# Sums of squares added in pairs on GpSimd, weight splits cut in halves, and attention values as products of two heads

## The chip, the cores and the metric

One core of a Trainium2 chip runs the whole program in one launch. The metric is the device time of that core in microseconds. Five engines work side by side, each through its own list of instructions, and wait for one another on semaphores: TensorE (PE in the profile, its weight loads as PEld), VectorE (DVE), ScalarE (ACT), GpSimd (POOL) and SyncE (SP), which issues most of the DMAs.

## What is computed

Four layers over 4 sequences of 256 tokens with 256 features: a product with a context matrix whose operands are rounded to fp8, a feed-forward layer with ternary weights, a cross attention with int8-rounded weights (16 heads), and a block with grouped attention (32 query heads, 8 key and value heads, head size 64, causal) and a mixture of 16 experts. The change touches the second layer and the attention of the fourth. Cut to these two:

```python
def _L0_ffn_ref(x, w_gate_up, w_proj):          # x: layer norm of the residual
    gu = jnp.einsum('bsd,hd->bsh', x, ternary_quant(w_gate_up))
    gate, up = jnp.split(gu, 2, axis=-1)        # 1024 hidden features each
    h = jax.nn.silu(gate) * up
    hn = h * rsqrt(mean(h * h, -1) + eps)
    return jnp.einsum('bsh,dh->bsd', hn, ternary_quant(w_proj))

def _L1_ffn_ref(x, ...):                        # its attention
    q, k, v = h @ wq, h @ wk, h @ wv            # 32, 8, 8 heads of 64
    scores = einsum('bqhd,bkhd->bhqk', rope(q), rope(k)) / 8    # causal
    o = einsum('bhqk,bkhd->bqhd', softmax(scores), v)
    x = x + o @ wo
    ...
```

## The kernel before

All data that is worked on stays in SBUF, most of it in one large tensor, `arena`, whose stretches are named by hand. Every engine's order is written out by hand in its own block (`sync`, `gpsimd`, `scalar`, `vector`, `tensor`); a semaphore is raised by the instruction that makes a value and waited for by those that use it.

**The first feed-forward layer.** The tokens are taken in two chunks of 512 (`CHUNKS`), the 1024 hidden features in 8 blocks of 128 (`J0`). That gives 16 units `u`, chunk `u // 8`, block `u % 8`. In a unit:
- TensorE (`gate_and_up`, line 1743) makes gate and up of the block, 8 products of 512 columns, in two of four PSUM banks. It waits until the product of unit u-2 is formed.
- ScalarE takes the silu of gate (line 937), and then for the unit before (`h0_hi`) rounds the product to float16 (line 928) and squares it (line 931) into a ring of two, `h_sq`.
- VectorE multiplies silu by up into `h0` (line 1320).
- GpSimd subtracts the rounded half from the product (line 733), which gives the low half.
- TensorE sums the squares of unit u-2 over the features (`sum_squares`, line 1752): for each of 4 token tiles a product of the 128x128 squares, as the weights, with a column of ones. In float32 that is two records each.

After unit 9 stands the down product of chunk 0 (`ffn0_down(0)`, line 1765, 64 products of 256 columns), which needs the low halves of units 0 to 7; after the last sums stands that of chunk 1. At unit 11 VectorE takes the mean square of chunk 0 (`mean_square`, line 1308), GpSimd raises it to the power -1/2 (line 744; in GpSimd's list this stands after unit 9's operations), and VectorE scales and adds the down product to the residual (`add_ffn0`, line 1299) and takes statistics (line 1132). For chunk 1 the same follows after VectorE's rounding of the int8 weights of the next layer (`q8`, lines 1156 to 1173).

Within the same units five pieces of the fourth layer's weights (`FW = 5`, 2048 columns each) are loaded into two staging buffers and split into a float16 high and low half. SyncE issues the load of piece i (line 632) when the split of piece i-2 is done. GpSimd makes the high half (line 739, "the cast") in the units `FW_AT = [4, 6, 8, 10, 12]`, behind the unit's subtraction; VectorE makes the low half (line 1328, "the split") two units later (`FW_LAG`), behind the unit's product. The lists in question:

```python
            for i in range(FW):
                if i == 0:
                    sp.wait_ge(w0_cast, 2 * PIECES)
                if i >= 2:
                    sp.wait_ge(fw_ready, i - 1)
...
                if u == J0 + 3:
                    mean_square(0)
                    add_ffn0(0)
                if u - FW_LAG in FW_AT:
```

**The grouped attention** has 64 units (`UNITS`): batch, group of 4 query heads (`GH`) that share a key and value head, and query tile `t` of 128 tokens; with causal masking tile 0 sees one key tile and tile 1 two. In step i TensorE does, in this order: `a_turn(i-2)` (transposes of the weights of attention, line 1982), `a_score(i)` (lines 1965 to 1967), a projection of later tokens (line 1800), `a_values(i-2)` (line 1999) and `out_projection(i-3)` (line 2015). `a_values` multiplies, for each pair of heads, key tile and head in the pair, a 128x64 block of values, as weights, with 128 columns of `apt`; even heads fall on the lower 64 partitions of PSUM bank 5, odd ones on the upper 64. All of it is float32, two records for each product.

## Time and profile before

| | us |
|---|---|
| median of 3 runs | 794.15 (793.99 to 794.79) |
| the profiled execution | 799.23 |
| its span, first to last instruction | 797.4 |

Mean granted clock of TensorE over the span: 0.917 of full speed. Engines' busy times: TensorE 632.0, VectorE 557.4, GpSimd 463.4, ScalarE 431.2 us.

Times in the views are microseconds from the start of the span, with durations in ns where said. A line of a timeline is: start, duration, engine, source line, operation, output <- input by the program's names, size, count of the instructions merged, and in brackets the idle time of the engine before it and what ended that. A matmul's record ends when the modelled pipeline is through; the next one of its kind starts earlier.

### The profile page before, as it was taken

The page shows a single profiled execution, that of the slowest core. Times are in us where ns is not written, and L with a number is a line of the kernel's source. Part 1 is how long each engine was busy: PE and PEld are TensorE (multiplying, and loading weights), DVE is VectorE, ACT ScalarE, POOL GpSimd, SP SyncE. Part 2 cuts the span into 40 slices and gives each one's busy share as a digit, 9 for nine tenths or more (in the row PEclk, how much of TensorE's full clock was granted, in tenths as well). Part 3 has the DMA queues.
Part 4 walks back from the last instruction along what each step waited for, and adds up shares of the span by engine and source line. Part 5 has one row for each costly group of instructions (what it writes and reads, how often), then busy time and mean ns, then how long its engine had stood idle before and what let it go on. Part 6 is the DMA issues. An engine that isn't in the chain of part 4 may idle for free.

```text
span 797.4 us, 16336 instructions
## 1 busy us (share of the span) xinstructions
PE 632.0 (79%) x5656; PEld 441.5 (55%) x5656; DVE 557.4 (70%) x1420; ACT 431.2 (54%) x1213; POOL 463.4 (58%) x424
## 2 busy tenths in 40 slices
PE   0247999468888844689999999999887789999970
PEld 0124667246566533367777777677675436666640
DVE  5999558868878976856677577677656765555445
ACT  4823532059768820456576666666654217777640
POOL 1051654248977942269698788768532336777750
PEclk9778896789999976989999999999999979999995
DMA  9500130127536530024042332422500913333428
GB/s 299 189 1 1 49 110 1 53 79 221 168 118 207 158 121 1 0 54 80 15 89 46 93 55 42 67 28 50 177 15 8 401 47 96 105 108 109 103 84 263
DMA packets 83466, 77.99 MB, mean 98 GB/s; under 512 B 49408, under 2 KB 75776, under 8 KB 82880
## 3 DMA queue, kind: packets, MB, share of 16 engines
q1 hardware_dynamic: 78880, 64.33, 28.0%
q0 software_dynamic: 4512, 12.71, 5.5%
q8 instruction: 42, 0.69, 0.4%
q14 instruction: 32, 0.26, 0.1%
HBM read 47.46 MB, written 18.55 MB: 83 GB/s over the span
## 4 chain that ended last, share of the span: by engine, by line
PE 52%; DVE 24%; ACT 7%; POOL 7%; issue 6%; DMA 2%; SPq 1%; POOLq 0%; ACTq 0%; DVEq 0%
PE ps L1800 10%; PE ps L2093 8%; PE ps L2015 5%; PE ps L1999 5%; PE ps L1982 5%; PE ps L2116 4%; ACT arena L974 2%; PE ps L1765 2%; PE ps L1857 2%; DVE arena L1496 2%; PE ps L1743 2%; POOL arena L832 2%; DVE tiny L1489 2%; PE ps L1724 2%; ACT arena L1059 1%
## 5 line engine op out<-in xcount | busy, mean ns | idle before, releaser
L1059 ACT ACTIVATE arena<-ps,tiny 128x128 f32<-128x128 f32 (+1 forms) x256 | 104.2, 419 | 53.6 <-DVE tiny L1489 53.6
L832 POOL TENSOR_TENSOR arena<-arena,tiny 128x512 f32<-128x512 f32 x64 | 93.9, 1467 | 62.9 <-DVE tiny L1500 62.6
L1496 DVE COPY arena<-ps 128x512 f32<-128x512 f32 x64 | 44.3, 691 | 75.3 <-PE ps L1982 75.3
L2093 PE MATMUL ps<-arena 128*128 (+1 forms) x282 | 68.7, 380 | 1.0 <-DVE arena L1640 0.5
L1800 PE MATMUL ps<-arena,xt_hi 128*128 128x512 f16 (+1 forms) x224 | 64.2, 372 | 3.6 <-DVE xt_lo L1278 3.0
L867 POOL DMA_INDIRECT arena<-h_store,arena x47 | 46.0, 979 | 33.5 <-DVE arena L1619 19.5
L1999 PE MATMUL ps<-arena 128*64 128x128 f32 x768 | 56.1, 280 | 11.3 <-DVE arena L1504 11.3
L1489 DVE TENSOR_REDUCE tiny<-ps 128x4 f32<-128x512 f32 x64 | 60.9, 952 | 1.3 <-PE ps L1967 0.9
L1999 PEld LDWEIGHTS ps<-arena 128*64 128x64 f32 x768 | 41.4, 136 | 32.3 <-issue 23.1
L1633 DVE SCALAR_TENSOR_TENSOR ps<-ps,arena 128x256 f32<-128x256 f32 x47 | 20.3, 433 | 55.4 <-ACT arena L1111 55.4
L1965 PE MATMUL ps<-arena 128*128 128x128 f16 (+1 forms) x256 | 58.5, 247 | 0.2 <-ACT arena L1038 0.2
L1967 PE MATMUL ps<-arena 128*128 128x128 f16 (+1 forms) x256 | 58.5, 247 | 0.0
L873 POOL DMA_INDIRECT y_store<-arena x47 | 46.4, 987 | 20.1 <-issue 12.2
L974 ACT ACTIVATE arena<-arena 128x256 f32<-128x256 f32 x128 | 54.6, 506 | 2.7 <-DVE arena L1395 2.6
L2015 PE MATMUL ps<-arena 128*128 128x256 f16 x384 | 53.0, 274 | 2.6 <-DVE xn L1511 2.4
L1982 PE MATMUL ps<-ident,arena 128*128 128x128 f32 x384 | 53.0, 274 | 2.3 <-POOL arena L832 2.3
L820 POOL TENSOR_TENSOR arena<-arena 128x512 f16<-128x512 f32 x36 | 41.7, 1158 | 21.2 <-ACT arena L1028 11.8
L1059 ACT ACTIVATION_READ_ACCUMULATOR arena<-ps,tiny 128x1 f32 x256 | 52.0, 203 | 0.0
L1966 PE MATMUL ps<-causal,ident_bf 128*128 128x128 bf16 x256 | 51.6, 220 | 0.0
L826 POOL TENSOR_TENSOR arena<-arena 128x512 f32<-128x512 f32 x34 | 43.2, 1270 | 7.3 <-DVE arena L1471 7.1
L1395 DVE CUSTOM_DVE_ANT_0 arena<-ps,arena 128x256 f32<-128x256 f32 x128 | 46.6, 420 | 0.0
L1982 PEld LDWEIGHTS ps<-ident,arena 128*128 128x128 f32 x384 | 43.4, 141 | 5.7 <-POOL arena L832 5.1
(295 smaller groups left out, 1738.4 us busy)
## 6 DMA issues: line engine op xcount, KB each, us to landing
e_store<-arena SPq DMA_DIRECT2D x13, 768.0 KB, 4.3
arena<-e_store SPq DMA_DIRECT2D x13, 768.0 KB, 9.4
work<-w_dram SPq DMA_DIRECT2D x27, 256.0 KB, 4.6
xn<-w_dram SPq DMA_DIRECT2D x21, 256.0 KB, 4.7
arena<-w_gate_up_t_dram SPq DMA_DIRECT2D x2, 1024.0 KB, 8.9
arena<-wq_dram SPq DMA_DIRECT2D x2, 1024.0 KB, 7.4
arena<-wo_dram SPq DMA_DIRECT2D x2, 1024.0 KB, 5.8
work<-y_store SPq DMA_DIRECT2D x8, 256.0 KB, 5.2
```

The source lines that it names most:

```text
L832: nc.gpsimd.tensor_tensor(p, p, arec[:, u % 4, :].unsqueeze(2).broadcast_to([P, GH, L]), ALU.mult)\
L974: nc.scalar.activation(xp[:, i % 2, h, :], masked[:, i % 2, h, :], ACT.Exp, bias=xnm[:, i % 4, h:h + 1], scale=-1.0).then_inc(x_exp, 1)
L1059: nc.scalar.activation(ap_[u % 3][:, h, 0:L], head_scores(u, h), ACT.Exp, bias=anm[:, u % 4, h:h + 1], accum_out=asum[:, u % 4, h:h + 1]). ...
L1489: nc.vector.tensor_reduce(anm[:, u % 4, :].rearrange("p (m h) -> p m h", m=u % TB + 1), scores, AX.X, ALU.max, negate=True).then_inc(a_max, 1)
L1496: nc.vector.tensor_copy(apt[:, u % 2, 0, :], ps[:, 3, :]).then_inc(a_pt, 1)
L1800: last = mm(dst, l, r, start=(n == 0), stop=(n == 3 * len(pairs) - 1))
L1965: mm(dst, q, kat[b % 2][:, g, 0:L], start=True, stop=False)
L1967: last = mm(dst, q, kbt[b % 2][:, g, 0:L], start=False, stop=True)
L1982: last = nc.tensor.transpose(ps[:, 3 + k, h * P:(h + 1) * P], ap_[u % 3][:, h, k * P:(k + 1) * P], ident[:, :])
L1999: last = mm(ps[half * HD:(half + 1) * HD, 5, pair * P:(pair + 1) * P], av[b % 2][:, k, g * HD:(g + 1) * HD], apt[:, u % 2, k, h * P:(h + 1 ...
L2015: last = mm(ps[:, 6, t * D:(t + 1) * D], l, r[:, g * 2 + o, :], start=first, stop=final)
L2093: last = mm(ps[:, 2 + i % 2, :], xg[:, i % 2, x_half * KB + k, :], weights(hidden_weights(slot, w_half, k), i), start=(n == 0), stop=(n == 5))
```

## The change

Three edits.

1. ScalarE squares into a ring of four (`h_sq` moves to another stretch of `arena`). After every second unit's subtraction GpSimd adds the squares of the two units, in place. `sum_squares` takes pairs: 8 calls instead of 16, at the units 4, 6, ... 14; pair 6 follows the last unit, and pair 7 stands inside the second down product, after its second token tile.
2. VectorE's split of a weight piece becomes two instructions of 1024 columns: the first two units after the cast, the second three units after, each behind what else VectorE does in its unit. The count of `fw_ready` doubles: SyncE waits for both halves of the piece whose buffer it fills.
3. `a_values` takes both pairs of heads in one product: 256 columns in two strided blocks of 128, instead of two products of 128. The order becomes key tile, then even and odd heads.

```diff
@@ -222,9 +222,9 @@
 
         h_hi, h_lo = ([c0([J0, CHUNK], F16), t[:, :, :].rearrange("p t d -> p (t d)").bitcast(F16)
                        .rearrange("p (j n) -> p j n", j=J0)] for t in (work, work2))
-        h_sq = c0([2, CHUNK], F32)
         w_sg = c0([PIECES, 2048], BF16)
         silu0 = c0([2, CHUNK], F32)
+        h_sq = carver(36864, 38912)([4, CHUNK], F32)
         h0 = carver(0, 4096)([J0, CHUNK], F32)
 
 
@@ -382,6 +382,7 @@
         h0_hi_ready = sem("h0_hi_ready")
         h0_split = sem("h0_split")
         h0_squared = sem("h0_squared")
+        squares_added = sem("squares_added")
         ms_out = sem("ms_out")
         ffn0_out = sem("ffn0_out")
         ms0_ready = sem("ms0_ready")
@@ -627,7 +628,7 @@
                 if i == 0:
                     sp.wait_ge(w0_cast, 2 * PIECES)
                 if i >= 2:
-                    sp.wait_ge(fw_ready, i - 1)
+                    sp.wait_ge(fw_ready, 2 * (i - 1))
                 for dst, src in stage_parts(a, i):
                     sp.dma_start(dst, src).then_inc(stage_loaded[i % 2], 16)
             sp.wait_ge(ffn0_added, CHUNKS)
@@ -732,6 +733,10 @@
                 pool.wait_ge(h0_hi_ready, u + 1)
                 nc.gpsimd.tensor_tensor(h_lo[c][:, j, :], h0[:, j, :], h_hi[c][:, j, :], ALU.subtract)\
                     .then_inc(h0_split, 1)
+                if u % 2:
+                    pool.wait_ge(h0_squared, u + 1)
+                    nc.gpsimd.tensor_tensor(h_sq[:, u % 4 - 1, :], h_sq[:, u % 4 - 1, :], h_sq[:, u % 4, :], ALU.add)\
+                        .then_inc(squares_added, 1)
                 if u in FW_AT:
                     i = FW_AT.index(u)
                     pool.wait_ge(w0_ready, PIECES)
@@ -926,9 +931,9 @@
             def h0_hi(u):
                 act.wait_ge(h0_ready, u + 1)
                 nc.scalar.activation(h_hi[u // J0][:, u % J0, :], h0[:, u % J0, :], ACT.Copy).then_inc(h0_hi_ready, 1)
-                if u >= 2:
-                    act.wait_ge(ms_out, u - 1)
-                nc.scalar.activation(h_sq[:, u % 2, :], h0[:, u % J0, :], ACT.Square).then_inc(h0_squared, 1)
+                if u >= 4:
+                    act.wait_ge(ms_out, u // 2 - 1)
+                nc.scalar.activation(h_sq[:, u % 4, :], h0[:, u % J0, :], ACT.Square).then_inc(h0_squared, 1)
 
             for u in range(U0):
                 act.wait_ge(gate_up, u + 1)
@@ -1304,7 +1309,7 @@
                     stat(c * TC + t, x)
 
             def mean_square(c):
-                vec.wait_ge(ms_out, (c + 1) * J0)
+                vec.wait_ge(ms_out, (c + 1) * J0 // 2)
                 nc.vector.tensor_scalar(ms0, ps[:, 6 + c, 0:TC], 1.0 / H0, FFN_EPS, ALU.mult, ALU.add)\
                     .then_inc(ms0_ready, 1)
                 vec.wait_ge(inv0_ready, c + 1)
@@ -1322,11 +1327,14 @@
                 if u == J0 + 3:
                     mean_square(0)
                     add_ffn0(0)
-                if u - FW_LAG in FW_AT:
-                    i = FW_AT.index(u - FW_LAG)
-                    vec.wait_ge(fw_hi_ready, i + 1)
-                    nc.vector.scalar_tensor_tensor(stage_target(i, False), stage[:, i % 2, :], WS,
-                                                   stage_target(i, True), ALU.mult, ALU.subtract).then_inc(fw_ready, 1)
+                for part in range(2):
+                    if u - FW_LAG - part in FW_AT:
+                        i = FW_AT.index(u - FW_LAG - part)
+                        cols = slice(part * 1024, (part + 1) * 1024)
+                        vec.wait_ge(fw_hi_ready, i + 1)
+                        nc.vector.scalar_tensor_tensor(stage_target(i, False)[:, cols], stage[:, i % 2, cols], WS,
+                                                       stage_target(i, True)[:, cols], ALU.mult, ALU.subtract)\
+                            .then_inc(fw_ready, 1)
                 if u < 4:
                     next(projection_steps, None)
             vec.wait_ge(xw_loaded, 64)
@@ -1745,12 +1753,13 @@
                             n += 1
                 last.then_inc(gate_up, 1)
 
-            def sum_squares(u):
-                c, j = u // J0, u % J0
-                pe.wait_ge(h0_squared, u + 1)
+            def sum_squares(pair):
+
+                c, j = pair // (J0 // 2), pair % (J0 // 2)
+                pe.wait_ge(squares_added, pair + 1)
                 for t in range(TC):
-                    last = mm(ps[:, 6 + c, t:t + 1], h_sq[:, u % 2, t * P:(t + 1) * P], ones_col[:, :],
-                              start=(j == 0 and t == 0), stop=(j == J0 - 1 and t == TC - 1))
+                    last = mm(ps[:, 6 + c, t:t + 1], h_sq[:, 2 * pair % 4, t * P:(t + 1) * P], ones_col[:, :],
+                              start=(j == 0 and t == 0), stop=(j == J0 // 2 - 1 and t == TC - 1))
                 last.then_inc(ms_out, 1)
 
             def ffn0_down(c):
@@ -1766,15 +1775,16 @@
                                       w_bf[:, 2, j * D:(j + 1) * D], start=(n == 0), stop=(n == 2 * J0 - 1))
                             n += 1
                     last.then_inc(ffn0_out, 1)
+                    if c and t == 1:
+                        sum_squares(U0 // 2 - 1)
 
             for u in range(U0):
                 gate_and_up(u)
-                if u >= 2:
-                    sum_squares(u - 2)
+                if u >= 4 and u % 2 == 0:
+                    sum_squares(u // 2 - 2)
                 if u == J0 + 1:
                     ffn0_down(0)
-            sum_squares(U0 - 2)
-            sum_squares(U0 - 1)
+            sum_squares(U0 // 2 - 2)
             ffn0_down(1)
 
             pe.wait_ge(ffn0_added, CHUNKS)
@@ -1915,7 +1925,7 @@
             pe.wait_ge(xo_added, T)
             transpose_tokens(3, work)
             pe.wait_ge(xt_ready, 16)
-            pe.wait_ge(fw_ready, FW)
+            pe.wait_ge(fw_ready, 2 * FW)
             def project(n):
                 b, c, t, _ = SIDE[n]
                 past = [m for m in range(n) if SIDE_BANK[m] == SIDE_BANK[n]]
@@ -1992,13 +2002,11 @@
                     pe.wait_ge(a_pt2, u // 2 + 1)
                 if u:
                     pe.wait_ge(a_o_read, u)
-                for pair in range(GH // 2):
-                    for k in range(t + 1):
-                        for half in range(2):
-                            h = pair * 2 + half
-                            last = mm(ps[half * HD:(half + 1) * HD, 5, pair * P:(pair + 1) * P],
-                                      av[b % 2][:, k, g * HD:(g + 1) * HD], apt[:, u % 2, k, h * P:(h + 1) * P],
-                                      start=(k == 0), stop=(k == t))
+                for k in range(t + 1):
+                    pairs = apt[:, u % 2, k, :].rearrange("p (a half q) -> p a half q", half=2, q=P)
+                    for half in range(2):
+                        last = mm(ps[half * HD:(half + 1) * HD, 5, 0:2 * P], av[b % 2][:, k, g * HD:(g + 1) * HD],
+                                  pairs[:, :, half, :], start=(k == 0), stop=(k == t))
                 last.then_inc(a_o, 1)
 
             def out_projection(u):
```

## Rows read from the trace of the kernel before

**Rows 1.** The page, part 1: busy us, share of the span, instructions.

```profile
PE 632.0 (79%) x5656; PEld 441.5 (55%) x5656; DVE 557.4 (70%) x1420; ACT 431.2 (54%) x1213; POOL 463.4 (58%) x424
```

**Rows 2.** Busy time by stretch: stretch, us, each engine busy (instructions), clock, DMA.

```profile
99.40:130.00 30.60, 27.94 (x175) 19.96 (x175) 20.77 (x24) 12.20 (x23) 19.27 (x12) 0.88 0.24 75
345.00:615.00 270.00, 253.20 (x2527) 191.89 (x2525) 183.45 (x370) 171.82 (x646) 194.00 (x153) 1.00 0.29 60
```

**Rows 3.** The chain that ended last, 110 to 146 us: start, us, what.

```profile
113.58 1.03 POOL inv L744
...
140.32 0.89 DVE x L1299 x2
```

**Rows 4.** Timeline of TensorE in the first feed-forward layer.

```profile
99.42 7.15 PE L1765 MATMUL ps<-arena 128*128 128x256 bf16 x64 [0.81 <-POOL arena L733]
...
110.67 0.95 PE L1752 MATMUL ps<-ones_col,arena 128*128 128x1 f32 x8
...
121.25 1.70 PE L1752 MATMUL ps<-ones_col,arena 128*128 128x1 f32 x8
...
130.41 9.87 PE L1765 MATMUL ps<-arena,work 128*128 128x256 bf16 x64
```

**Rows 5.** Timeline of GpSimd in the first feed-forward layer.

```profile
88.85 1.16 POOL L733 TENSOR_TENSOR arena<-arena 128x512 f16<-128x512 f32 x1 [1.38 <-ACT arena L928]
...
98.12 1.16 POOL L733 TENSOR_TENSOR arena<-arena 128x512 f16<-128x512 f32 x1
99.23 3.21 POOL L733 TENSOR_TENSOR work<-arena,work 128x512 f16<-128x512 f32 x1
...
117.57 1.15 POOL L733 TENSOR_TENSOR work<-arena,work 128x512 f16<-128x512 f32 x1
...
121.85 1.89 POOL L739 TENSOR_SCALAR arena<-arena 128x2048 f16<-128x2048 f32 x1
...
127.38 2.27 POOL L733 TENSOR_TENSOR work<-arena,work 128x512 f16<-128x512 f32 x2 [2.52 <-ACT work L928]
```

**Rows 6.** Timeline of VectorE in the first feed-forward layer.

```profile
98.19 3.24 DVE L1328 SCALAR_TENSOR_TENSOR arena<-arena 128x2048 f16<-128x2048 f32 x1 [1.61 <-POOL arena L739]
...
109.57 3.26 DVE L1328 SCALAR_TENSOR_TENSOR arena<-arena 128x2048 f16<-128x2048 f32 x1
112.76 0.68 DVE L1320 TENSOR_TENSOR arena<-ps,arena 128x512 f32<-128x512 f32 x1
...
116.33 1.41 DVE L1132 BATCH_NORM_STATS2 stats<-x 128x6 f32<-128x256 f32 x4
...
126.94 0.68 DVE L1320 TENSOR_TENSOR arena<-ps,arena 128x512 f32<-128x512 f32 x1
127.54 1.74 DVE L1161 TENSOR_REDUCE wamax<-arena 128x6 f32<-128x1536 f32 x1
...
138.08 0.88 DVE L1299 SCALAR_TENSOR_TENSOR x<-ps,inv,x 128x256 f32<-128x256 f32 x2 [1.14 <-POOL inv L744]
```

**Rows 7.** Timeline of SyncE's queue, 111 to 142 us.

```profile
112.86 0.37 SPq L632 DMA_DIRECT2D arena<-wo_dram  x1
```

**Rows 8.** The page, part 6: DMAs by name, KB each, us to landing.

```profile
arena<-wo_dram SPq DMA_DIRECT2D x2, 1024.0 KB, 5.8
```

**Rows 9.** Groups by line and form, 345 to 615: busy us, mean ns.

```profile
L1999 PE MATMUL ps<-arena 128*64 128x128 f32 x768 | 56.1, 280 | 11.3 <-DVE arena L1504 11.3
...
L2015 PE MATMUL ps<-arena 128*128 128x256 f16 x383 | 52.9, 274 | 2.6 <-DVE xn L1511 2.4 <-DVE arena L1504 0.2
...
L826 POOL TENSOR_TENSOR arena<-arena 128x512 f32<-128x512 f32 x34 | 43.2, 1270 | 7.3 <-DVE arena L1471 7.1
...
L1965 PE MATMUL ps<-arena 128*128 128x128 f16 x124 | 22.4, 219 | 0.0
```

**Rows 10.** Busy time of a stretch; its granted clock comes before DMA.

```profile
129.20:136.02 6.82, 6.82 (x34) 5.20 (x35) 6.65 (x23) 1.13 (x2) 0.46 (x1) 0.50 0.00 1
```

**Rows 11.** Timeline of TensorE: one unit of values with two key tiles.

```profile
612.49 1.09 PE L1999 MATMUL ps<-arena 128*64 128x128 f32 x16 [1.54 <-DVE arena L1504]
```

## The prediction

> **What bounds the kernel now.** I read the page first: TensorE is busy 79% of the span, GpSimd 58% [rows 1]. A share is a mean over stages, so next comes the table by stretch. The edits touch two: the first feed-forward layer (68 to 143 us), and the grouped attention (345 to 615 us), where TensorE is busy 253.2 of 270 us [rows 2], so only TensorE time counts there. In the first layer no engine is full, so I read the chain of waits: it runs through GpSimd's power at 113.58 and, after the second down product, VectorE's last additions at 140.32 [rows 3]. Then the timelines, engine by engine. The reader is to see four things.
>
> First, TensorE waits for GpSimd at the first down product (0.81 us, then 7.15 us of work) [rows 4]. GpSimd stands on the path by unit 7 already.
>
> Second, GpSimd and VectorE exclude each other in some pairs of operations. A subtraction takes GpSimd 1.16 us, but the one at 99.23 took 3.21 and ended at 102.44, 1.0 us after VectorE's split (98.19 to 101.43); that split in turn took 3.24 us, having waited for the subtraction of 98.12 to end at 99.28, so it needs some 2.15 alone [rows 5, 6]. I count each GpSimd operation and each split as holding one shared turn.
>
> Third, the last weight piece. Its load is issued at 112.86, when split 2 (109.57 to 112.83) is done, and lands 5.8 us later, at 118.7; its cast begins at 121.85, so the load is covered with 3.1 us to spare [rows 5 to 8].
>
> Fourth, the end: VectorE computes the eight tensors of the int8 weights from 127.54, is ready at 138.08, and adds the last pair of tiles at 140.32, after TensorE [rows 3, 6]. So VectorE's slack is about 1.4 us.
>
> **The change part by part.** *Squares in pairs.* TensorE issues 64 instead of 128 one-column records: eight groups fewer. A group of 8 spans 0.95 us at 2.4 GHz, some 0.8 of it not hidden, and 1.70 at the lower clock [rows 4]. That is 6 to 7 us of TensorE work, but this engine waits in this layer, so the work leaves only if nothing else is late. Added are eight additions of 128x512 float32 on GpSimd; no such addition runs in this layer, the nearest row is the float32 addition in attention, 1.27 us each [rows 9]. Bounds: 1.16 (the mixed subtraction) and 1.5 (with some exclusion on top). I take 1.27. Of these, the one after unit 3 has cover: GpSimd stood idle 1.38 us before 88.85 [rows 5]. The one after unit 5 delays subtraction 7, for which the first down product waits; the missing sums bring TensorE's units forward, and the split cut in two lets GpSimd in between. I work out +0.5 us for the start of that product (between 0 and +1.3).
>
> *Split in halves.* Split 2 becomes part 0 at unit 10 and part 1 at unit 11. Product 11, at 112.76 now behind the whole split [rows 6], starts half a split earlier: 112.3 with the +0.5 above. But part 1 stands in VectorE's order behind the mean square, the four additions and the four statistics of unit 11. Those additions need the inverse from GpSimd, whose power now stands behind the addition of squares 8 and 9 (112.3 to 113.6), so it starts at 113.6, as before (113.58). The statistics end at 117.7 as before [rows 3, 6]. Part 1 then waits for subtraction 11 to end (117.57 + 1.15 = 118.7 [rows 5]) and runs 1.1 us: done at 119.9, where split 2 was done at 112.83. SyncE issues the last load only then: **7.1 us later**. Nothing else is queued behind it on SyncE until the layer's end. It lands at 119.9 + 5.8 = 125.7. The cast of 121.85 starts at 125.9: **+4.0 us**, a new wait. Queued behind it on GpSimd: subtractions 13, 14, 15 and the additions of squares; waiting for it on VectorE: split 4, with product 15 behind its first part.
>
> The sum from there, in turns of the shared resource: cast 1.9 (127.8), subtraction 13 1.15 (128.9), split 4 part 0 1.1 (130.0; product 15 then, 126.94 before, +3.1), addition 13 1.27 (131.3), part 1 1.1 (132.4), subtractions 14 and 15 2.3 (134.7). Before, subtraction 15 ended at 127.38 + 2.27 = 129.65 [rows 5]: **+5.0**. The second down product starts at 134.8, where it started at 130.4 behind the last sums: +4.4. It lasted 9.87 us [rows 4], of which 5.6 at the lower clock, since 129.2 to 136.0 is granted 0.50 [rows 10]. TensorE will stand idle for longer before it than it did, so I give it no more of the full clock than it had. Inside it now stands one group of sums: +0.8. TensorE's end: 134.8 + 9.9 + 0.8 = 145.5, against 130.41 + 9.87 = 140.28: +5.2. VectorE, from 132.4 instead of 127.54, is ready for its last pair at 138.08 + 4.85 + 0.9 = 143.8 and is covered. So the layer ends **5.2 us later**. If the down product ran wholly at 2.4 GHz (7.15 us as the first one [rows 4]), VectorE would end it at 143.8: +3.5. If it ran wholly at the lower clock (about 14.3 + 1.6): +10. After it comes the layer norm on VectorE with every engine waiting, so nothing gives this back.
>
> *Values as products of two heads.* The records of that line fall from 768 to 384, each twice as wide. A unit of 16 takes 1.09 us, a record every 0.055 us [rows 11]. What a record costs is seen from its kind: 128 float32 columns last 280 ns, about as long as 256 float16 columns (274), while 128 float16 columns last 219 [rows 9]. A float32 column costs two; 128 of them hold their part of the array 256/2.4 = 107 ns. As one starts every 55 ns, the two halves of the output (64 columns each) are at work side by side. Afterwards 8 records hold their half 512/2.4 = 213 ns each, two at a time: 4 x 0.213 = 0.85 against 8 x 0.107 = 0.86. Only the 1 to 2 ns between records fall by half: 10 ns less for each of 32 units with two key tiles, 5 ns for the other 32, 0.5 us. Bounds: 0 and, if the offset of one half against the other grows with the record, +3; I take -0.4.
>
> A rule speaks otherwise. By the Trainium skill, "TensorE: Matmul & The Clock Gate", section "LDWEIGHTS (loading the stationary operand)", a weight load takes its columns divided by 1.2 GHz, 53 ns for 64; by that rule 16 loads in line fill 0.85 us, and the trace's loads of a unit fit that as well as the streams do. If loads are the limit, halving them pays; that is the first rival, which is priced from rows below.
>
> **Sum.** +5.2 - 0.4 = +4.8 us. The profiled execution takes 799.23 us (span 797.4 and 1.8 around it), 5.1 above the median of the runs, 794.15. The difference is carried over: profile 804.0, median 794.15 + 4.8 = **799.0 us**.
>
> **The rivals.** *Loads are the limit in attention (faster).* Then a unit of 16 saves 8 x 0.055 = 0.44 us and one of 8 saves 0.22: 32 x 0.66 = 21 us of TensorE. The line is busy 56.1 us and TensorE is full 94% of the stretch, so of the 21 perhaps half to two thirds reach the end, as other engines become late: -10 to -14. With +4.8 from the first layer: about 787. For it: the fit at 55 ns. Against it: the equal times of 128 float32 and 256 float16 columns, which the rule does not give. It decides from 5 us of attention saved. Chance 0.10.
>
> *The load is not late (no change).* If part 1 of split 2 came before the additions in effect, or the load landed in 3 us, the cast would start at 122.5; the adds would cost 2 x 1.27 less what the halves release early, and TensorE's lighter load would pay the rest: the layer at -1 to +1.5, 793 to 795.7. Against it: the order of the statements is fixed. Chance 0.15.
>
> *The clock.* The adds leave TensorE idle for longer, and the second down product, or units 14 and 15 also, run at the lower clock throughout: +8 to +10 in the layer, 801 to 804. Chance 0.15.
>
> *The exclusion does not bind the addition of squares*, or the halves slip between: +3 to +4, 797 to 798; within my case.
>
> **How the numbers follow.** My case, 796.5 to 801: 0.58. The clock: 0.15. No change: 0.15. Loads: 0.10, and 0.02 for neither. The likeliest is 799.0. The range takes in my case, the clock's and part of the no-change case: 793.8 to 803.0, leaving out loads (0.10) and the edges (0.08). A measurement can tell about 0.2% (1.6 us) from no change. Slower by more, above 795.7: 0.76. Faster by more, below 792.6: 0.12. Same: 0.12.
>
> **What would show it.** In the changed profile: the last load issued at about 120 instead of 112.86, and VectorE's split 2 part 1 just before it; GpSimd's last cast at about 126, after idle time that ends with a DMA; the additions of squares at about 1.27 us; the second down product starting near 134.8; the last pair of additions near 145.5. In attention: 384 records of about 0.38 us, a unit of 8 in about 1.1 us, and the stretch from the projections to the last product as long as now within 1 us. I am wrong if the last load is issued before 116, if a unit of values takes under 0.8 us, or if subtraction 15 ends by 131.

## The result and the profile after

The changed kernel takes 801.68 us, median of 7 runs (797.76 to 803.08), against 794.79 us (793.99 to 796.69) for the kernel before on the same chip: a ratio of 1.0079, interval 1.0059 to 1.0100, which is +6.3 us (4.7 to 8.0). Timed again with the experiments below the ratio is 1.0068 (1.0044 to 1.0092), +5.4 us. The prediction was 799.0 us, +4.8, with a range of 793.8 to 803.0; the median lies in the range, 2.7 above its middle value. Two executions, one of the kernel before at 1281 us and one of the kernel "values, casts on ScalarE" at 2137 us, are in none of the ratios.

The medians hide a shape. In the timings with the experiments 11 of 35, 6 of 34 and 6 of 24 executions of the kernel before took over 797.5 us, the others 793 to 797; of the 19 of after one took 797.8, two took 796.5, and 16 took 800 or more. The lowest times are only 3.6 to 3.8 us apart (793.99 and 797.76, 792.83 and 796.46). So part of the 5 to 6 us may be that executions of 798 us and more become the rule; the mean granted clock of an execution doesn't sort them (the kernel before took 799.47 at 0.928 and 792.96 at 0.919), and what does is not shown.

The first profile of the changed kernel took 802.12 us (span 800.3), only 2.9 more than the profile of before, 799.23. Both kernels were therefore profiled a second time: 795.64 us (span 793.8) for before, 804.8 (span 802.9) for after. One profile of either kernel differs from the next by 2 to 4 us, so sizes are taken from all of them. Part 1 of the page of after, to be set against [rows 1], and its part 5 for the values:

```profile
PE 625.4 (78%) x5208; PEld 414.6 (52%) x5208; DVE 561.2 (70%) x1425; ACT 431.2 (54%) x1213; POOL 477.4 (60%) x432
...
L2008 PE MATMUL ps<-arena 128*64 128x256 f32 x384 | 55.6, 394 | 11.4 <-DVE arena L1512 11.4
```

TensorE is busy 6.6 us less and the kernel is slower. GpSimd does 14.0 us more. By line, GpSimd in the first layer (60 to 150 us; columns as in [rows 9]), after and then before:

```profile
L738 POOL TENSOR_TENSOR arena<-arena 128x512 f32<-128x512 f32 x8 | 16.0, 2002 | 0.0
L734 POOL TENSOR_TENSOR work<-arena,work 128x512 f16<-128x512 f32 x8 | 11.9, 1488 | 6.1 <-ACT work L933 6.1
```

```profile
L733 POOL TENSOR_TENSOR work<-arena,work 128x512 f16<-128x512 f32 x8 | 12.9, 1620 | 8.1 <-ACT work L928 8.1
```

Eight additions of squares take 16.0 us, 2.0 each and not 1.27. The distribution of that line says why: 1.26 us at the least, 2.25 in the median.

```profile
L738 POOL TENSOR_TENSOR arena<-arena x8: 1261/2246/2252, 79.4 to 133.2; 128x512 f32<-128x512 f32 x8
```

Five of the six long ones stand beside half a split of VectorE. The sixth, that of unit 1, stands beside an operation of VectorE with two inputs in `arena` (start, length, engine, line), and ends 1.13 us after it:

```profile
79.37 2.25 POOL L738 TENSOR_TENSOR arena<-arena 128x512 f32<-128x512 f32 x1
```

```profile
79.04 1.45 DVE L1219 TENSOR_TENSOR arena<-arena 128x2048 bf16<-128x2048 bf16 x1
```

The chain of waits of after, from the power to the end of the layer (start, length, what; [rows 3] are its answers in before):

```profile
113.33 1.02 POOL inv L749
...
114.38 1.67 DVE x L1304 x4
...
117.44 2.11 DVE arena L1335
...
119.57 5.08 DMA arena<-wo_dram
...
124.80 1.90 POOL arena L744
126.70 1.12 POOL work L734
127.82 2.21 POOL arena L738
130.03 3.22 POOL work L734 x2
133.25 0.14 issue
133.38 6.55 PE ps L1774 x32
139.94 0.79 PE ps L1761 x8
140.72 3.53 PE ps L1774 x32
...
144.28 0.89 DVE x L1304 x2
```

The reader is to see the predicted path, link by link: power, additions of unit 11, part 1 of split 2, then a DMA that was not in the chain of before in this layer, the last cast, three subtractions with an addition between them, the second down product with a group of sums inside. The timelines confirm the two waits: SyncE issues the last load at 119.57 (112.86 in before [rows 7]; the line below merges it with the load issued at 101.28 and ends with it at 119.94), and GpSimd is idle 2.03 us for it.

```profile
101.28 18.66 SPq L633 DMA_DIRECT2D arena<-wo_dram  x2
```

```profile
124.80 1.90 POOL L744 TENSOR_SCALAR arena<-arena 128x2048 f16<-128x2048 f32 x1 [2.03 <-DMA arena<-wo_dram]
```

All the kernels' profiles side by side, in microseconds after the layer's first product (the one at 68.14 in the profile of before); "end" is the end of the layer's last statistics. The first three rows are one and the same layer, since the edit of the values does not touch it; they show how far two profiles of one thing lie apart. Where ScalarE casts, "last cast" is the start of the second half; the first half starts at 48.0 and at 53.8.

| kernel | first down product | last load issued | last cast | subtraction 15 ends | second down product | end | runs, ratio to before |
|---|---|---|---|---|---|---|---|
| before | 31.3 | 44.7 | 53.7 | 61.5 | 62.3 | 74.5 | |
| before, again | 29.6 | 43.0 | 52.0 | 59.7 | 60.8 | 71.9 | 1.0024 (0.9999 to 1.0048) |
| values alone | 31.8 | 45.3 | 54.3 | 62.1 | 62.7 | 75.1 | 1.0003 (0.9975 to 1.0031) |
| **after** | 30.0 | 51.4 | 56.6 | 65.1 | 65.2 | 78.4 | 1.0079 (1.0059 to 1.0100) |
| **after, again** | 30.4 | 51.7 | 57.2 | 65.6 | 65.8 | 77.9 | 1.0068 (1.0044 to 1.0092) |
| halves alone | 31.7 | 51.1 | 56.5 | 63.7 | 64.2 | 76.1 | 1.0026 (0.9999 to 1.0052) |
| pairs alone | 30.0 | 43.7 | 54.3 | 62.8 | 62.9 | 75.8 | 1.0063 (1.0043 to 1.0083) |
| pairs alone, narrow additions | 28.6 | 42.2 | 51.4 | 59.1 | 59.2 | 71.4 | 0.9999 (0.9978 to 1.0020) |
| after, halves early | 30.0 | 46.3 | 55.8 | 64.2 | 64.4 | 76.5 | 1.0027 (1.0004 to 1.0050) |
| after, narrow additions | 28.9 | 49.9 | 55.3 | 62.7 | 62.9 | 75.4 | 1.0032 (1.0012 to 1.0052) |
| after, both | 26.7 | 40.8 | 48.3 | 56.7 | 56.8 | 69.9 | 1.0015 (0.9992 to 1.0037) |
| values, casts on ScalarE | 28.6 | 42.0 | 50.4 | 58.4 | 59.4 | 71.2 | 0.9994 (0.9970 to 1.0019) |
| after, casts on ScalarE | 28.4 | 48.1 | 56.3 | 65.0 | 65.1 | 78.3 | 1.0070 (1.0044 to 1.0095) |

The span less this layer's length is 720.8 to 723.4 us in twelve of the thirteen profiles, and 725.0 in the second one of after. So the differences between profiles are made in this layer. But an old profile has to be chosen with care: those of "before" and "values alone" took 799.2 and 799.9 us, some 4 above the medians of their kernels, and have layers of 74.5 and 75.1; "before, again" took 795.6, like the median, and has 71.9. Beside after's 78.4 (an execution of 802.1, median 801.7) the layer grew by 6.5 us, which is all of the loss; against the mean of the three old profiles it is 4.3.

### The profile page after: what moved, and what is told of

Read it like the earlier page. It is cut to its first block, busy times and chain, and to the rows that moved or that the text cites. A ratio compares the mean times of both kernels' runs of the same rounds, so it can differ in the third digit from the quotient of the medians.

```text
span 800.3 us, 15453 instructions
## 1 busy us (share of the span) xinstructions
PE 625.4 (78%) x5208; PEld 414.6 (52%) x5208; DVE 561.2 (70%) x1425; ACT 431.2 (54%) x1213; POOL 477.4 (60%) x432
## 4 chain that ended last, share of the span: by engine, by line
PE 50%; DVE 26%; POOL 9%; ACT 7%; issue 5%; DMA 2%; SPq 1%; POOLq 0%; DVEq 0%; ACTq 0%
PE ps L1810 9%; PE ps L2101 8%; PE ps L2023 5%; PE ps L1992 5%; PE ps L2008 5%; PE ps L2124 4%; PE ps L1774 2%; ACT arena L979 2%; PE ps L1867 2%; DVE arena L1504 2%; POOL arena L837 2%; DVE tiny L1497 2%; ACT arena L1064 1%; PE ps L2113 1%; PE ps L2076 1%
## 5 line engine op out<-in xcount | busy, mean ns | idle before, releaser
L2008 PE MATMUL ps<-arena 128*64 128x256 f32 x384 | 55.6, 394 | 11.4 <-DVE arena L1512 11.4
L1992 PE MATMUL ps<-ident,arena 128*128 128x128 f32 x384 | 53.0, 274 | 2.3 <-POOL arena L837 2.3
L1976 PE MATMUL ps<-causal,ident_bf 128*128 128x128 bf16 x256 | 51.7, 220 | 0.0
L2023 PEld LDWEIGHTS ps<-arena 128*128 128x128 f16 x384 | 32.3, 98 | 30.2 <-issue 26.8
L1867 PE MATMUL ps<-ident,arena 128*128 128x128 f32 x256 | 37.1, 292 | 13.0 <-DVE arena L1423 8.3
```

Of the source, the lines that this page charges most:

```text
L1992: last = nc.tensor.transpose(ps[:, 3 + k, h * P:(h + 1) * P], ap_[u % 3][:, h, k * P:(k + 1) * P], ident[:, :])
L2008: last = mm(ps[half * HD:(half + 1) * HD, 5, 0:2 * P], av[b % 2][:, k, g * HD:(g + 1) * HD], pairs[:, :, half, :], start=(k == 0), stop=(k ...
L2023: last = mm(ps[:, 6, t * D:(t + 1) * D], l, r[:, g * 2 + o, :], start=first, stop=final)
```

## The experiments

**One edit at a time.** The theory: the loss is made in the first layer, by the additions' turns and by the last load; the values change nothing. The rivals: the values gain or cost microseconds (weight loads are the limit, or the two halves of the output stop overlapping), or one of the two edits in the layer costs all of it. First the values alone:

```diff
-                for pair in range(GH // 2):
-                    for k in range(t + 1):
-                        for half in range(2):
...
+                for k in range(t + 1):
+                    pairs = apt[:, u % 2, k, :].rearrange("p (a half q) -> p a half q", half=2, q=P)
+                    for half in range(2):
```

> The kernel before with the third edit alone: values of attention as products of two heads, 256 columns. My theory (a float32 record of 256 columns costs what two of 128 do): -0.5 us, between -1 and +1, and in the profile 384 records of about 0.38 us, a unit of two key tiles in 1.1 us. Rival A (this edit makes part of the slowdown, because the halves of the array work side by side for less of the time): +2 us or more, a unit above 1.2 us. Rival B (weight loads are the limit): -10 us, a unit of 0.7 us.

Measured: 795.87 us against 795.51, ratio 1.0003. The line's records take 55.6 us instead of 56.1, and the stretch from the first to the last of them is 261.7 us here and in both profiles of after, where it is 262.0 in both of before: -0.3 us, as worked out. Busy time of the weight loads of this line in attention, before and after:

```profile
L1999 PEld LDWEIGHTS ps<-arena 128*64 128x64 f32 x768 | 41.4, 136 | 32.3 <-issue 23.1 <-DVE arena L1496 9.2
```

```profile
L2008 PEld LDWEIGHTS ps<-arena 128*64 128x64 f32 x384 | 23.7, 135 | 35.9 <-issue 23.2 <-DVE arena L1504 9.3
```

384 loads are gone and the time stays, so they lay under the streams. By the rule of the Trainium skill ("TensorE: Matmul & The Clock Gate", section "LDWEIGHTS (loading the stationary operand)") a load takes its columns over 1.2 GHz; an estimate by it is 0.85 us for the 16 loads of a unit and 0.43 for 8. The unit went from 1.09 us to 1.08, so loads at that price are not what bounds it: the trace speaks against the first rival of the prediction.

The splits in halves alone:

```diff
-                if u - FW_LAG in FW_AT:
-                    i = FW_AT.index(u - FW_LAG)
...
+                for part in range(2):
+                    if u - FW_LAG - part in FW_AT:
```

> The kernel before with the second edit alone: splits in halves, the second part of split 2 behind the additions and statistics of unit 11. My theory (the last load is issued late and the last cast waits for it): +2.5 us (1.5 to 3.5), the last load issued at about 119 instead of 112.9, GpSimd idle before the last cast with a DMA as what ended it. Rival (only the additions of squares on GpSimd cost time): 0, and a gain of up to 1 us since product 15 no longer stands behind a whole split.

Measured: ratio 1.0026, +2.1 us (0 to 4); the medians lie 3.5 us apart, 798.98 and 795.51, and 11 of the 12 executions took over 798, while the lowest, 793.40, is 0.5 above the lowest of before. The theory of the expectation came out: the load at 119.52 us, GpSimd idle 2.71 us before the cast and released by the DMA, and the cost in the range. The last load is issued 51.1 us into the layer, as late as in after, and the last cast starts at 56.5, as in after. By the ratio this is a third of the loss, with a wide interval. So the late load, which the prediction made the origin of nearly all of it, is most likely not that by itself.

The squares in pairs alone:

```diff
+                if u % 2:
+                    pool.wait_ge(h0_squared, u + 1)
+                    nc.gpsimd.tensor_tensor(h_sq[:, u % 4 - 1, :], h_sq[:, u % 4 - 1, :], h_sq[:, u % 4, :], ALU.add)\
+                        .then_inc(squares_added, 1)
```

> The kernel before with the first edit alone: squares added in pairs on GpSimd, splits whole. My theory (additions take turns with VectorE's splits and stand ahead of subtractions that TensorE waits for): +3 us (1.5 to 5), the last load issued near 113 and the cast not waiting for it; the second down product starts some 3 us later than in the kernel before. Rival (the late load alone makes the slowdown): 0 or a gain of 1 us, from TensorE's lighter load.

Measured: ratio 1.0063, +5.0 us (3.4 to 6.6), the top of the range expected, with no load late (43.7). The second down product starts at 62.9, some 2 later than in the second profile of before and 1 later than the mean of the three, not the 3 us expected. Its additions wait for whole splits, where those of after wait for halves: 3.31 us in the median. GpSimd from 87 to 100 us of this kernel (start, length, engine, line, operation):

```profile
87.82 1.91 POOL L744 TENSOR_SCALAR arena<-arena 128x2048 f16<-128x2048 f32 x1
89.70 1.15 POOL L734 TENSOR_TENSOR arena<-arena 128x512 f16<-128x512 f32 x1
90.81 3.31 POOL L738 TENSOR_TENSOR arena<-arena 128x512 f32<-128x512 f32 x1
94.09 1.16 POOL L734 TENSOR_TENSOR arena<-arena 128x512 f16<-128x512 f32 x1
95.21 1.89 POOL L744 TENSOR_SCALAR arena<-arena 128x2048 f16<-128x2048 f32 x1
```

From cast to cast pass 7.39 us. The casts of before in the same stretch:

```profile
96.26 1.90 POOL L739 TENSOR_SCALAR arena<-arena 128x2048 f16<-128x2048 f32 x1
...
102.41 1.89 POOL L739 TENSOR_SCALAR arena<-arena 128x2048 f16<-128x2048 f32 x1
```

They are 6.15 us apart, and that is full already: a cast of 1.90, a split of 2.15 and two subtractions of 1.16 are 6.4 us of turns, less the hundredths by which records overlap. An addition of 1.26 comes on top: 7.4. The layer has three such cycles from cast to cast, 7.37 to 7.39 us here and 6.15 to 6.17 in before: 3.7 us of the loss.

**The additions' price.** In the next run they keep their place, their waits and their order, but have 32 columns instead of 512; the kernel leaves out the sums of the other columns:

```diff
-                    nc.gpsimd.tensor_tensor(h_sq[:, u % 4 - 1, :], h_sq[:, u % 4 - 1, :], h_sq[:, u % 4, :], ALU.add)\
+                    nc.gpsimd.tensor_tensor(h_sq[:, u % 4 - 1, 0:32], h_sq[:, u % 4 - 1, 0:32], h_sq[:, u % 4, 0:32], ALU.add)\
```

> The kernel before with the squares added in pairs, splits whole and values as before, and the additions narrowed from 512 columns to 32 (the rest of the sum is left out). It prices the time of eight additions where no load is late. If the additions cost by the time that they hold the turn shared with VectorE, the ratio falls from 1.0063 for the full additions to 0.998 to 1.002, since TensorE's lighter load (64 records fewer) is then free of charge. Rival, the waits by pairs (squares reach TensorE two units later, one group of sums inside the second down product): the ratio stays at 1.004 or above.

Measured: ratio 0.9999 where the full additions gave 1.0063. Eight times 1.01 us of GpSimd, 8 us, make some 5.1 us of the kernel. The cycles from cast to cast are 6.35 to 6.38 us again. What is left of the edit, the waits by pairs and TensorE's 64 fewer records, comes to nothing together (-1.8 to +1.6 us); the run doesn't part them, so a small cost of the one and a small gain of the other may cancel. The "6 to 7 us of TensorE work" in any case don't appear in the time. GpSimd in this kernel, and one split of VectorE:

```profile
89.33 1.16 POOL L734 TENSOR_TENSOR arena<-arena 128x512 f16<-128x512 f32 x1
90.44 2.30 POOL L738 TENSOR_TENSOR arena<-arena 128x32 f32<-128x32 f32 x1
92.70 1.16 POOL L734 TENSOR_TENSOR arena<-arena 128x512 f16<-128x512 f32 x1
```

```profile
89.39 3.24 DVE L1333 SCALAR_TENSOR_TENSOR arena<-arena 128x2048 f16<-128x2048 f32 x1 [1.28 <-POOL arena L744]
```

This is the turn at its plainest. The split is issued at 89.39, behind the subtraction of 89.33; it works when that ends, at 90.49, for 2.15 us, and ends at 92.63. The addition of 32 columns takes 0.25 us where nothing stands in its way; here it takes 2.30 and ends 0.11 us after the split. By the Trainium skill, "SBUF — State Buffer", section "Who interferes with whom", a VectorE instruction with two SBUF inputs contends with a GpSimd instruction that reads SBUF, and the port pair that they share is an exclusive lock. The trace agrees, to a tenth of a microsecond.

The same narrowing in the changed kernel:

> The changed kernel with GpSimd's additions of squares narrowed from 512 columns to 32; it leaves out the sum of the squares for the other columns of one unit in each pair, and every instruction, order and wait stays. It prices the time of the additions apart from their order. If the time that an addition holds the turn shared with VectorE is a cost of its own beside the late load, the additions last some 0.1 to 0.3 us, the power starts near 112.3 (113.33 in the changed kernel), subtraction 15 ends 1.5 to 2.5 us sooner than 133.2, and the ratio to the kernel before falls from 1.008 to about 1.005. Rival, the late load alone: it is still issued near 119, the cast still starts near 124.5, and the ratio stays at 1.008. Rival, the additions alone: the ratio falls to that of the halved splits by themselves, 1.0026, or below.

Measured: ratio 1.0032, so -2.9 to -3.7 us against the two timings of after. Subtraction 15 ends at 131.3, 1.9 sooner, as the theory had it; the late load alone (1.008) falls, the additions alone (1.0026) are within the interval, and so is the 1.005 that the theory gave. The load is still late (49.9), and GpSimd, with less to add, waits for it longer than in after.

```profile
123.92 1.90 POOL L744 TENSOR_SCALAR arena<-arena 128x2048 f16<-128x2048 f32 x1 [2.65 <-DMA arena<-wo_dram]
```

The power starts at 112.31 us, as expected (112.3).

**The late load's price.** The changed kernel with VectorE's order changed, the halves ahead of the mean square and the additions:

```diff
+                for part in range(2):
+                    if u - FW_LAG - part in FW_AT:
...
                 if u == J0 + 3:
                     mean_square(0)
                     add_ffn0(0)
```

> The changed kernel with one move: in VectorE's list the splits of a unit stand ahead of the mean square and the additions of unit 11, so the last load is issued at about 113 again. My theory: a gain of 1 to 2.5 us on the changed kernel, still 3 to 5 us above the kernel before, as the additions on GpSimd stay. If the late load were the whole of it: within 1 us of the kernel before. If the clock were the whole of it: no gain.

Measured: ratio 1.0027, -3.3 to -4.1 us against after, more than the 1 to 2.5 expected; what is left above before, 2.1 us (0.3 to 4.0), is less than the 3 to 5 expected. The load is issued 5 us sooner (46.3), but the cast starts only 0.8 to 1.4 us sooner (55.8), and no longer behind a DMA: GpSimd is filled to that point by its own turns.

```profile
119.58 2.25 POOL L738 TENSOR_TENSOR arena<-arena 128x512 f32<-128x512 f32 x1
121.79 2.14 POOL L734 TENSOR_TENSOR work<-arena,work 128x512 f16<-128x512 f32 x1
123.90 1.89 POOL L744 TENSOR_SCALAR arena<-arena 128x2048 f16<-128x2048 f32 x1
```

Both together:

> The narrowed additions (32 of 512 columns, the rest of the sum left out, as in the run before this) together with the halves of a split put ahead of the mean square and the additions of unit 11 on VectorE. Both suspected costs are then gone. If the additions' time and the late load are all that the change costs, the last load is issued near 113.5, the last cast starts by 123, subtraction 15 ends by 131, and the ratio to the kernel before is 0.998 to 1.001 (1.0027 with the full additions). If there is a third cost, in TensorE's order (one group of sums inside the second down product) or in the waits for pairs, the ratio stays at 1.003 or above.

Measured: ratio 1.0015 (0.9992 to 1.0037), a little above the range expected and not to be told from before, although its profile has the shortest layer of all (69.9). Either cure alone takes 3 to 4 us off the 5.4 to 6.3, both together 4.2 to 5.1. Each of these differences is uncertain by some 2 us; as they stand, the two causes overlap. The waits fit that: with less to add, GpSimd waits 2.65 us for the load instead of 2.03. A third cost of up to 2.9 us, the upper end of the interval, is not excluded by this run.

**Another relief of the turn.** If GpSimd and VectorE share one resource, five casts of 1.90 us taken out of it should pay. On the kernel before, with the values' edit:

```diff
-                if u in FW_AT:
...
-                    nc.gpsimd.tensor_scalar(stage_target(i, True), stage[:, i % 2, :], WS, 1.0, ALU.mult, ALU.mult)\
...
+                for part in range(2):
+                    if u - part in FW_AT:
...
+                        last = nc.scalar.activation(stage_target(i, True)[:, cols], stage[:, i % 2, cols], ACT.Copy, scale=WS)
```

> The kernel before with the values of two heads in one product, and with the casts of the weight pieces moved from GpSimd (1.90 us each, in turn with VectorE's splits) to ScalarE, in two halves of 1024 columns behind the squares of two units. If the turn shared by GpSimd and VectorE bounds the end of this layer, five casts of 1.90 us leave it, subtraction 15 ends about 1 to 3 us before 129.66, and the time is 0.5 to 3 us below the kernel before (ratio 0.997 to 0.999). Rival: ScalarE takes the bound, since the casts then stand ahead of the squares and halves of the next units: ratio above 1.001. Rival: TensorE's own units bound the layer by then, and what GpSimd gives up is idle: ratio 0.999 to 1.001.

Measured: ratio 0.9994 (0.9970 to 1.0019): no gain that can be told. GpSimd now has gaps of 4 to 5 us that end with ScalarE, one of them here, so GpSimd is no longer what the layer waits for.

```profile
107.05 1.16 POOL L733 TENSOR_TENSOR work<-arena,work 128x512 f16<-128x512 f32 x1 [4.61 <-ACT work L922]
```

This kernel has a wait of its own, though: ScalarE stands idle for the last load, and its chain runs through that load.

```profile
116.31 1.06 ACT L941 ACTIVATE arena<-arena 128x1024 f16<-128x1024 f32 x1 [3.76 <-DMA arena<-wo_dram]
```

So the run doesn't show that relief of the turn is worth nothing: what it gave may have gone into this wait.

The same edit on the changed kernel. (The expectation says ten casts; there are five, in ten halves.)

> The changed kernel with the casts of the weight pieces on ScalarE, in two halves of 1024 columns behind the squares of two units, as in the run of the kernel before with that edit (ratio 0.9994). Ten casts of 1.90 us leave the turn shared by GpSimd and VectorE, where eight additions came in. If the loss is that turn together with the late load, whose cast no longer stands in GpSimd's order ahead of subtractions 13 to 15, most of it goes: ratio 1.000 to 1.004, subtraction 15 ends 62 to 63 us after the layer's first product (65.1 in the changed kernel). If the loss lies in VectorE's order alone (part 1 behind the additions of unit 11), ScalarE waits for the late load in place of GpSimd, and squares and halves wait behind it: ratio 1.006 or above.

Measured: ratio 1.0070, no better than after. The rival holds: part 1 still stands behind the additions, the load is issued at 48.1, and now ScalarE waits for it, 8.78 us, with the gates and squares of the next units queued behind.

```profile
121.98 1.06 ACT L946 ACTIVATE arena<-arena 128x1024 f16<-128x1024 f32 x1 [8.78 <-DMA arena<-wo_dram]
```

A reading that fits both kernels: a late load costs what the engine that waits for it would have done meanwhile, and ScalarE stands ahead of every unit. How much of the 1.0070 the additions of squares still add was not separated here.

**The same kernels again.**

> The kernel before once more, unchanged, for a second profile and for the spread of its own times. Ratio 1.000 (0.998 to 1.002). The first profile took 799.23 us where the median of the runs is 795. If the profiler adds these 4 us, this one takes 799 again, with the first layer 74.5 us long and the attention 262; if they are one way in which the granted clock falls in an execution, this one may take 794 to 796, and the difference lies in stretches that were granted 0.50 in the one profile and 1.00 in the other.

> The changed kernel once more, unchanged, for a second profile. Two profiles of the kernel before have a first layer of 74.49 and 71.92 us, so one pair of profiles can't size the loss. If the loss is the late load, it is there in every profile: the last load is issued 6 to 8 us after split 2 would have ended whole (119 to 120), the second down product starts 65 us after the layer's first product (65.22 in the first profile; 62.27 and 60.76 in the two of before), and the ratio is 1.006 to 1.010. If the first profile caught an unlucky fall of the clock, this one has a layer of 75 us or less and the ratio is below 1.005.

Measured: before 795.64 us in the profile, layer 71.9; after 804.8, layer 77.9, ratio 1.0068. The late load and the start of the second down product repeat within 0.6 us in after; in before the layer came out 2.6 us shorter. Windows of TensorE in the two profiles of before (bounds, length, busy, granted clock, DMA share, GB/s), the first and then the second:

```profile
78.00:88.00 10.00, 10.00 (x44) 0.66 0.00 0
...
128.00:138.00 10.00, 10.00 (x61) 0.66 0.00 1
```

```profile
78.00:88.00 10.00, 10.00 (x54) 0.83 0.00 0
...
128.00:138.00 10.00, 10.00 (x71) 0.77 0.01 2
```

TensorE is busy without a gap in all four, and does 44 records in the one and 54 in the other: that goes with the granted clock, 0.66 against 0.83. The 0.17 between them is 1.7 us of full clock over these ten, an estimate, and the first down product starts 1.7 us sooner. The second profile took 795.64 us, so the 4 us between the first one and the median are not the profiler's; 2.6 of the 3.6 us between the two profiles lie in this layer. Before's runs spread over 793 to 802 us; whether all of that is the clock was not separated.

## Why the prediction was right, and where it was not

The forecast of a slower kernel held, by the two mechanisms named in it (turns with VectorE, and a load issued 7 us later), and the size is in the range. How it divided the loss between the two is not borne out, so that the sum came out near is in part luck.

Means of the three profiles with the old layer and of the two of after, in microseconds after the layer's first product, against the prediction's steps.

- *Values, -0.4.* Right: -0.3 in the profiles; the runs, 1.0003 (0.9975 to 1.0031), can't tell so little. A unit of 8 takes 1.08 us (about 1.1 predicted), a record 0.379 us (0.38). Both rivals fell, the weight loads and the halves that no longer overlap.
- *Additions at 1.27 us.* Right as a turn held, wrong as a record. Two of the eight records took 1.26 us; the other six took 2.25, five beside a half split and one beside VectorE's operation of line 1219, some 1.0 of it waiting. The step took the price of an operation alone from attention and gave the waiting no place in the record. What counts for the sum is not their 16.0 us but the turns they hold: the cost by narrowing them is 2.9 to 3.7 us in after and 5.1 where the splits are whole.
- *First down product, +0.5.* 30.2 against 30.9 in the mean, -0.7, outside the step's bounds (0 to +1.3) by a little; against the second profile of before, 29.6, it is +0.6. With unequal clocks in the units ahead of it, the profiles can't tell.
- *Power at 113.6, statistics end at 117.7, part 1 done at 119.9.* 113.33, 117.5 and 119.54: right, and with them the order on VectorE.
- *Last load +7.1, 5.8 us to land, last cast +4.0.* The load came 7.2 us later (51.6 against 44.3), landed in 5.1, and the cast started 3.6 later (56.9 against 53.3). Right as an event. **Only half right as the cause**: without additions the late load alone puts the cast at 56.5, 3.2 late, and with the load back in time the additions that stand before it in GpSimd's turns still put it at 55.8, 2.5 late. Either is nearly enough; beside the additions the load adds the last 1.1. The prediction priced this point by the latest arrival alone and did not ask where GpSimd would have been without it; it counted additions in turns only from the cast on.
- *Subtraction 15 +5.0, second down product +4.4, its length +0.8.* +4.3, +3.6, and +0.6 (9.9 us from its first to its last record against 9.3). Right within the spread of the profiles.
- *Layer +5.2.* +4.3 in the mean (78.2 against 73.8), +6.2 against the one old profile that took its kernel's median time (71.9). The runs say +5.4 to +6.3 for the kernel, so the step is right or a little low. The rest of the span doesn't hold the difference: it is 722.9, 721.9 and 723.0 us in the three old profiles and 721.9 and 725.0 in after's. Why the last one has 3 us more stays open.
- *The base of the sum.* The prediction took the profile of before, 5.1 above the median, for something to carry over: profile 804.0. After's first profile took 802.12, 0.4 above its median, and the second of before 795.64: the 5.1 were one execution's, not a constant.
- *The clock rival (+8 to +10).* In the first profiles of both kernels the second down product ran its first 6 us or so at 0.50 [rows 10]; the product of after is longer by 0.6 us in the mean, no more than its group of sums. The rival as priced fell. A lower clock elsewhere in the layer is not excluded: from 118 to 128 us the granted clock is 0.66 and 0.89 in the two profiles of before and 0.54 in the first of after, and what that costs was not separated.
- *"The load is not late".* It fell; but a kernel in which it is so (after, halves early) was still slower, by 0.27% (0.04 to 0.50), where the rival gave about no change: it let the lighter load of TensorE pay for the additions.

## What to carry to other kernels

Where two engines hold a resource in turns, add up the turns of a period before moving work onto either: here a cycle of 6.15 us held some 6 us of them, and eight additions of 1.26 us cost the kernel 5 us, although GpSimd was 58% busy over the span. Taking 64 records off an engine that waits gave nothing that could be told. A late arrival is to be priced against where the engine that waits would have been without it, not against where it was before the change; and cutting an operation in two moves its second half behind whatever stands next in its engine's order, together with every load that waits for it.

## What the runs showed of the hardware

- An addition of 128x32 float32 on GpSimd takes 0.25 us alone and 2.30 beside a split of 2048 columns; of 128x512, 1.26 alone, 2.25 beside a half split and 3.31 beside a whole one. The record is the waiting plus the operation's own work: both sizes waited about 1.0 us beside a half split (the narrow one took 1.23 there) and 2.05 beside a whole one.
- Sixteen records of 128 float32 columns take 1.09 us and eight of 256 take 1.08: halving the records and the weight loads of a line (41.4 to 23.7 us busy) left its time as it was.
- Two profiles of the same kernel gave one 74-us layer lengths 2.6 us apart, with granted clocks of 0.66 and 0.83 in the same ten microseconds of it. A difference of under 3 us in this stage can't be read from one pair of its profiles.
